# Convolution attention: values in column quarters, row sums as matmuls of their own, and a new order of the work around them

## The reference, cut to what matters

```python
def conv(x, ...):                                  # x: group norm of the input, (16, 128, 32, 32)
    q = einsum('bchw,oc->bohw', x, qW)             # 8 heads x 32, read as rows of 32
    k = einsum('bchw,oc->bohw', bn(dw_conv(x, kdwW, 2)), kW)     # 32 x 16 x 16
    v = einsum('bchw,oc->bohw', bn(dw_conv(x, vdwW, 2)), vW)
    attn = softmax(einsum('bnqd,bdl->bnql', q, k) / HEAD_DIM ** 0.5, axis=-1)   # over 256 keys
    ctx = einsum('bnql,bld->bnqd', attn, v)        # 8192 queries of an image, 32 values each
    return einsum('bchw,oc->bohw', ctx, oW)        # added to x
```

## Time and profile before

| | |
|---|---|
| time, median of 3 runs | 2161.94 us (2161.93 to 2164.02) |
| the profiled execution | 2174.15 us, its span 2172.4 us |
| PE, DVE, ACT busy | 1961.4, 1375.0, 989.7 us |
| mean granted TensorE clock | 0.967 |
| convolution attention | from 0 to 842.4 us of the span |

### The profile page before, as it was taken

How to read it: one execution, slowest core, us unless ns; L and a number is a source line. 1 busy time by engine, 2 the same in 40 slices (tenths; PEclk the granted TensorE clock), 3 DMA queues, 4 the chain that set the end, 5 groups by cost and what they waited for, 6 DMA issues and landing times. The chain is left out here.

```text
span 2172.4 us, 44335 instructions
## 1 busy us (share of the span) xinstructions
PE 1961.4 (90%) x11636; PEld 1466.1 (67%) x11636; DVE 1375.0 (63%) x3923; ACT 989.7 (46%) x2194; POOL 1029.3 (47%) x1367
## 2 busy tenths in 40 slices
PE   3999999999999998888898888887189999999997
PEld 2666666666666654665666666555189999999997
DVE  3676766767767665787788878876434444444443
ACT  0554555555455554444344333342045555555554
POOL 1221121212112111445554555555658888888887
PEclk9999999999999999999999999998589999999999
DMA  5322222222223222111111111111234444454454
GB/s 195 74 66 71 61 71 64 65 70 65 70 60 73 62 61 74 54 36 38 41 38 41 36 38 35 42 38 40 66 57 64 64 65 63 63 65 65 63 65 51
DMA packets 175423, 131.90 MB, mean 61 GB/s; under 512 B 33437, under 2 KB 164933, under 8 KB 175301
## 3 DMA queue, kind: packets, MB, share of 16 engines
q0 software_dynamic: 55808, 52.50, 15.1%
q1 hardware_dynamic: 118341, 77.16, 13.6%
q10 hardware_dynamic: 1152, 0.54, 0.1%
HBM read 31.47 MB, written 46.71 MB: 36 GB/s over the span
## 5 line engine op out<-in xcount | busy, mean ns | idle before, releaser
L1664 POOL DMA_INDIRECT out<-f_y,f_rows x272 | 424.1, 1559 | 45.5 <-POOL f_waited L1662 41.7
L447 DVE TENSOR_REDUCE neg_max<-s_bank 128x2 f32<-128x512 f32 x512 | 329.5, 685 | 133.5 <-PE s_bank L715 131.4
L1727 DVE SCALAR_TENSOR_TENSOR f_hidden<-f_silu,f_rows,f_h_bank 128x341 f32<-128x341 f32 x272 | 155.4, 571 | 307.6 <-ACT f_silu L1696 279.7
L567 ACT ACTIVATE probsT<-st_bank 128x512 f32<-128x512 f32 x512 | 276.6, 593 | 133.9 <-PE st_bank L733 133.6
L1096 POOL DMA_INDIRECT routed<-a_rows,a_target_idx x256 | 253.2, 989 | 68.6 <-issue 68.3
L335 POOL TENSOR_TENSOR waited<-nothing 128x1 int32<-128x1 int32 x64 | 12.1, 189 | 514.0 <-DVE q_low L436 514.0
L1473 PE MATMUL a_score_bank<-t_eT,t_gT 128*128 128x512 f32 x512 | 252.4, 617 | 1.2 <-DVE a_val L1140 1.2
L745 PE MATMUL o_bank<-probsT,v_ones 128*64 128x512 f32 x1024 | 248.0, 605 | 0.0
L1775 PE MATMUL f_y_bank<-w,f_hiddenT 114*128 (+1 forms) x1632 | 230.8, 277 | 1.3 <-ACT f_hiddenT L1688 1.3
L715 PEld LDWEIGHTS s_bank<-k_stack,q_stack 96*128 96x128 f32 x1024 | 141.9, 193 | 113.4 <-issue 94.0
L733 PE MATMUL st_bank<-q_stack,k_stack 98*128 98x512 f32 x512 | 214.0, 484 | 0.6 <-ACT probsT L567 0.5
(11 more groups left out here) (210 smaller groups left out, 3591.7 us busy)
## 6 DMA issues: line engine op xcount, KB each, us to landing
q_stack<-q_high SPq DMA_DIRECT2D x512, 64.0 KB, 2.3
f_rows<-routed SPq DMA_DIRECT2D x272, 66.0 KB
q_stack<-q_low POOLq DMA_DIRECT2D x256, 64.0 KB, 2.6
out<-X SPq DMA_DIRECT2D x16, 512.0 KB, 3.2
X<-in_x SPq DMA_DIRECT2D x1, 6144.0 KB, 22.1
out<-f_y,f_rows POOLq DMA_INDIRECT x272
q_stack<-max_rows SPq DMA_DIRECT2D x256, 4.0 KB
routed<-a_rows,a_target_idx POOLq DMA_INDIRECT x256
```

Of the source, the lines that this page charges most:

```text
L447: dve.tensor_reduce(neg_max[:, i % 2, CT * j:CT * (j + 1)], s_bank[h % 2][:], AX_X, ALU.max, negate=True).then_inc(max_ready, 1)
L567: act.activation(probsT[:, i % 2, c, lt, :], st_bank[lt][:], ACT.Exp).then_inc(exp_done, 1)
L1664: pool.indirect_dma_start(out=out, out_offset=bass.IndirectOffsetOnAxis(ap=rows[:, i, TOKEN:TOKEN + 1].bitcast(I32), axis=0), in_=y[:, i, ...
```

## The change

- The values go out in quarters: two pairs (an "octet", four chunks) at once, each chunk on 32 columns of its own quarter of `o_bank`. `values` runs in even iterations, for two pairs that are finished.
- The row sums come from matmuls of their own, `row_sums`, in odd iterations: the stationary operand has ones in one of 32 columns and zeros elsewhere, a different column for each octet of an image, and all four octets accumulate in one bank, `sum_bank`. Once per image ACT copies it out (`evacuate_sums`), PE turns it (`turn_sums`, end of i = 2) and DVE takes the reciprocals (`invert_sums`).
- The context is turned once per octet (end of odd iterations), and ACT, not DVE, takes it out (`evacuate_turned`, to `raw`). DVE scales half an image at a time (`scale`, i = 3 and i = 5 of the next period), and `project` of an image follows at i = 5 and i = 7 of the next period; `add_output` at i = 6 and at the end of i = 7.
- `m_bank` gives its bank to `sum_bank`; the maxes are turned into the first quarter of `c_bank`, with waits between the two uses.
- The convolution computes keys once and values, 64 columns, in two column halves at the same time (five taps and four); DVE adds the halves with a second operation. The copies of the keys are made in `split_keys`.
- `probsT` holds four pairs, `q_high` and `q_low` two groups of queries instead of four.
- On PE scores of rows 2 and 3 follow the second shifted scores at once; then come convolution or queries, then values or row sums, then a projection, then the turning. The statistics move to i = 2 (one half) and i = 4, `group_norm` to the end of i = 0.

```diff
+        sum_bank = ps("sum_bank", [P, COLS])
+        m_bank = c_bank[:, 0, :]
...
+                    dve.tensor_tensor(kv[:, slot, :], kv[:, slot, :], front[0:KV, 0:L], ALU.add).then_inc(kv_ready, 1)
...
+                def invert_sums(b):
+                    dve.wait_ge(sums_turned, b + 1)
+                    dve.reciprocal(rsum[:].rearrange("p (j c n) -> p j c n", j=OCTETS, c=OCTET_CHUNKS),
+                                   c_bank[:].rearrange("p n (c j) -> p j c n", j=QUAD)[:, 0:OCTETS]
+                                   ).then_inc(rsum_ready, 1)
+                    dve.wait_ge(rsum_ready, b + 1)
+                def scale(b, k):
+                    dve.wait_ge(c_out, OCTETS * (b + 1))
+                    wait(dve, out_full, 2 * (b - 1) + k + 1)
+                    part = slice(ROWS * k, ROWS * (k + 1))
+                    dve.tensor_tensor(context[:, part, :], raw[:, part, :],
+                                      rsum[:, part].unsqueeze(2).to_broadcast([P, ROWS, KD]), ALU.mult
+                                      ).then_inc(scaled, 1)
...
-                            normalise(*turned)
                         turning = pair(b, slot, i + LEAD - 1)
                         if has(turning[0]):
                             max_low(*turning)
+                        if i == 3 and has(b - 1):
+                            scale(b - 1, 0)
+                        if i == 5 and has(b - 1):
+                            scale(b - 1, 1)
+                        if i == 6 and has(b - 1):
+                            add_output(b - 1, 0)
...
+                        if i == 0 and has(new):
+                            group_norm(new)
+                        if i == 2 and has(b - 1):
+                            invert_sums(b - 1)
+                        if i == 2 and has(b + 2):
+                            half_stats(b + 2, 0)
+                        if i == 4 and has(b + 2):
+                            channel_stats(b + 2)
+                        if i == PAIRS - 1 and has(b - 1):
                             add_output(b - 1, 1)
-                        if i == PAIRS - 2 and has(b + 2):
-                            channel_stats(b + 2)
-                        if i == PAIRS - 1 and has(b):
-                            add_output(b, 0)
...
-                        wait(act, o_full, pair_no(b, i) - 1)
+                        wait(act, sums_full, octet_no(b, i // 2) - 1)
...
+                def evacuate_sums(b):
+                    act.wait_ge(sums_full, OCTETS * (b + 1))
+                    act.activation(sumT[:], sum_bank[:], ACT.Copy).then_inc(sums_out, 1)
+                def evacuate_turned(b, slot, o):
+                    act.wait_ge(c_full, octet_no(b, o) + 1)
+                    wait(act, scaled, 2 * b - (o < OCTETS // 2))
+                    rows = slice(2 * PAIR_ROWS * CT * o, 2 * PAIR_ROWS * CT * (o + 1))
+                    act.activation(raw[:, rows, :].rearrange("p (c n) d -> p n c d", c=OCTET_CHUNKS),
+                                   c_bank[:].rearrange("p n (c d) -> p n c d", d=KD), ACT.Copy).then_inc(c_out, 1)
...
-                            evacuate_context(*summed)
                         if i in Q_AT:
                             ahead, k = Q_AT[i]
                             if has(b + ahead):
                                 query_high(b + ahead, k)
+                        if i % 2 == 0 and has(summed[0]):
+                            evacuate_context(*summed)
+                        if i == 1 and has(b - 1):
+                            evacuate_sums(b - 1)
+                        if i % 2 and has(summed[0]):
+                            evacuate_turned(*summed)
...
+                    wait(pe, out_done, 2 * (b - 2))
...
+                    halves = ((4, 0, 1, 2, 7), (5, 3, 6, 8))
+                    for n in range(len(halves[0])):
+                        for part, taps in enumerate(halves):
+                            if n == len(taps):
+                                continue
+                            t = taps[n]
+                            di, dj = divmod(t, 3)
+                            out = front[KV * part:KV * (part + 1), 0:L].rearrange("p (i j) -> p i j", j=SIDE // 2)
+                            last = pe.matmul(out[:, di == 0:, dj == 0:], tap_w[:, t, :],
...
                     elif k == 2:
                         pe.wait_ge(q_low_done, Q_CHUNKS * b + 2)
+                        wait(pe, out_done, 2 * (b - 2) + 1)
...
-                    pe.wait_ge(ctx_done, pair_no(b, (k + 1) * PAIRS // 2 - 1) + 1)
-                    if k == 0 and has(b + 2):
-                        pe.wait_ge(gmean_ready, b + 3)
-                    elif k == 0 and has(b + 1):
-                        pe.wait_ge(q_low_done, Q_CHUNKS * (b + 1) + 3)
-                    elif k == 0:
-                        pe.wait_ge(head_done, head_no("e1"))
+                    pe.wait_ge(scaled, 2 * b + k + 1)
...
-                        for c in range(CHUNKS_PER_PAIR):
-                            last = pe.matmul(o_bank[HALF * c:HALF * (c + 1), :], v_ones[:, slot, lt, :],
-                                             probsT[:, i % 2, c, lt, :], start=(lt == 0), stop=(lt == LT - 1))
+                        for cc in range(OCTET_CHUNKS):
+                            i, c = divmod(cc, CHUNKS_PER_PAIR)
+                            last = pe.matmul(o_bank[QUAD * cc:QUAD * (cc + 1), :], v_rows[:, slot, lt, :],
+                                             probsT[:, (2 * o + i) % 4, c, lt, :], start=(lt == 0), stop=(lt == LT - 1))
...
+                def row_sums(b, o):
+                    if o == 0:
+                        wait(pe, sums_out, b)
+                    for lt in range(LT):
+                        for cc in range(OCTET_CHUNKS):
+                            i, c = divmod(cc, CHUNKS_PER_PAIR)
+                            last = pe.matmul(sum_bank[QUAD * cc:QUAD * (cc + 1), :], ones_at[:, o, :],
+                                             probsT[:, (2 * o + i) % 4, c, lt, :], start=(o == 0 and lt == 0),
+                                             stop=(o == OCTETS - 1 and lt == LT - 1), skip_group_check=True)
+                    last.then_inc(sums_full, 1)
+                def c_bank_free(b, i):
+                    turning = pair(b, 0, i + LEAD - 1)
+                    wait(pe, m_low_done, pair_no(turning[0], turning[2]) + 1 if has(turning[0]) else PAIRS * NB)
+                def turn_context(b, slot, o):
+                    pe.wait_ge(ctxT_full, octet_no(b, o) + 1)
+                    wait(pe, c_out, octet_no(b, o))
+                    wait(pe, rsum_ready, b)
                     for n in range(4):
-                        last = pe.transpose(c_bank[:, n, :], ctxT[:, i % 2, n * P:(n + 1) * P], ident[:])
+                        last = pe.transpose(c_bank[:, n, :], ctxT[:, o % 2, n * P:(n + 1) * P], ident[:])
                     last.then_inc(c_full, 1)
...
+                def turn_sums(b):
+                    pe.wait_ge(sums_out, b + 1)
+                    pe.wait_ge(c_out, OCTETS * (b + 1))
+                    for n in range(4):
+                        last = pe.transpose(c_bank[:, n, :], sumT[:, n * P:(n + 1) * P], ident[:])
+                    last.then_inc(sums_turned, 1)
...
-                        turned = pair(b, slot, i - 2)
-                        if has(turned[0]):
-                            turn_context(*turned)
+                        summed = octet(b, slot, i)
                         if has(scored[0]):
                             scores(*scored, 0)
                             scores(*scored, 1)
                         if has(turning[0]):
+                            if i == 3:
+                                wait(pe, rsum_ready, b)
+                            elif i % 2 == 0:
+                                before_last = octet(b, slot, i - 1) if i else octet(b - 1, 1 - slot, PAIRS - 1)
+                                if has(before_last[0]):
+                                    pe.wait_ge(c_out, octet_no(before_last[0], before_last[2]) + 1)
                             turn_maxes(*turning)
                         if has(b):
                             shifted_scores(b, slot, i, 1)
...
                             group_variances(new)
                         if i == PAIRS - 1 and has(b + 2):
                             group_means(b + 2)
...
-                        summed = pair(b, slot, i - 1)
-                        if has(summed[0]):
-                            values(*summed)
                         if has(scored[0]):
                             scores(*scored, 2)
                             scores(*scored, 3)
...
                             ahead, k = Q_AT[i]
                             if has(b + ahead):
                                 queries(b + ahead, k)
-                        if i == 3 and has(b - 1):
+                        if i % 2 == 0 and has(summed[0]):
+                            values(*summed)
```

(13 more changed lines are left out.)

194 lines of the change are left out of this document (94 added, 100 removed).

## The result

The changed kernel takes 2191.47 us (median of 4 executions, 2189.27 to 2194.87) against 2161.93 for the kernel before (4 executions, 2156.71 to 2164.02): a ratio of 1.0137, 95% interval 1.0115 to 1.016. It is slower by 1.4%, where 2148, 0.6% less, was forecast. The profiled executions stand 2193.1 to 2172.4 us in span.

What follows compares the result with a forecast made beforehand. PE sets the pace (busy 48.49 of 49.22 us per image). Iterations sum to 48.5 us, -0.65 per image, -10 us over 15 images; ends -4.0; about -14 in all, so 2161.94 goes to 2148; 8-in-10 range 2130 to 2203.

Steps and rivals of the forecast that it cites:

- the right two waits: Each iteration: row 3 of scores waits for DVE's row 1 bank, second shifted scores for exponentials; 0.41 us per iteration.
- leaves 41: Image 0: 48.5 less two projections, two blocks and 0.4 leaves 41 us against 47.43 before, so -6.4.
- +4.4: Stage end after the last values: 10.7 us after the change against 6.3 before.
- rival B: Values and row-sum blocks: quarters don't run four at once, 2203 to 2368; chances 0.13 (2167 to 2205), 0.10 above.
- Convolution and group means: Per image: convolution in column halves -1.6 us; idle gap at group means (i = 7) gone, -0.7 us.
- 2.7 us for the whole part: Each iteration from first shifted scores to end of rows 2 and 3's scores: 2.7 us, 2.29 without waits.
- Queries ahead of the block: Even iterations: queries, four records of 256 columns, add 0.85 us to the 4.57 of part and block.
- i = 3, "+0.15": DVE blocks on the turned sums at end of i = 2, making i = 3's first reduction 0.15 us late.
- i = 6, "+0.4": Queries at i = 6 wait for DVE's first half of the residual addition: 3.1 against 2.7 us, +0.4.
- C: ACT handovers or bank shared by maxes and context cost 0.3 us more in half the iterations: 2158 to 2167; chance 0.18.
- A: The forecast itself, whole kernel: 2148, with 2132 to 2157 for sizes within it; chance 0.47.
- D: Waits at rows of scores don't come: 3.3 us per image less, 2096, partly below 2130; chance 0.07.

Runs made afterwards that it cites:

- e10: Kernel before with only the column-halved convolution and the statistics in halves at i = 2 and i = 4; ratio 0.9866, image 46.78 us.
- e3: Changed kernel with two DVE steps reordered: half statistics ahead of reciprocals at i = 2, residual addition at start of i = 6; ratio 1.0066.
- e12: Changed kernel with each values or row-sums block in two halves, before the first scores and before the scores of rows 2 and 3; ratio 0.9869.
- e8: Changed kernel with the turned context copied out of PSUM by DVE at the start of even iterations, not by ACT; ratio 1.0092.
- e4: Kernel before with only the convolution in column halves and the statistics at i = 4; ratio 0.988.
- e1: Changed kernel with the block between second shifted scores and scores of rows 2 and 3, ACT's evacuations ahead of the queries'; ratio 1.0094.
- e5: e1 with the context turned right behind the row sums, plus e3's DVE order; ratio 1.0073.
- e11: e5 with each block in two halves and the reciprocals ahead of the statistics again at i = 2; ratio 0.9873.
- e9: Changed kernel with only the first half of each block moved, ahead of the first scores; second half stays behind convolution and queries; ratio 1.023.

## Why the prediction was wrong

The forecast had the right two waits and the wrong price for them, and so the wrong sign. The step that failed is the one that nets the gains of the convolution and the group means against the waits. All the rest of the change was put at +1.6 us per image by iterations (by terms +1.75: transposes -1.1, waits of the part +2.3, shared output bank and reciprocal +0.55); it costs +3.4 (e10 against after). The second step that failed is the ends, where "leaves 41" and "+4.4" carried the waits and the clock of a full image over to places that have less work to cover them.

Of the miss, 2191.5 - 2148 = 43.5 us, 34.7 lie in the span (2193.1 against 2172.4 - 14 = 2158.4). The other 8.8 are the step that took the profile's distance from the median (12.2 before) as unchanged; after, it is 3.4. The 2174.15 of the profile before isn't one of the four executions behind 2161.93; it lies beside that kernel's medians on two chips of this study (2175.14 and 2176.18) and not beside those on the two others (2158.5 and 2160.7), so the 12.2 may be a distance between chips. The chip of that profile isn't recorded.

- **Quarters (rival B): refuted, and the step was right.** Block 1.86 for 1.87. The Trainium skill (TensorE: Matmul & The Clock Gate, Part 3) measured 3.07 times for four tiles, there along the rows, which would have made an estimated 2.44 of a block. The trace doesn't bear that out for columns: four column quarters lose nothing to two halves.
- **Convolution and group means: right.** -2.4 alone (e10) for -2.3.
- **"2.7 us for the whole part": the mechanism was right, its terms too small.** Measured 2.81 (i = 4) and 2.88 (i = 5). By the maxes, i = 5: shifted scores 0.57 for my 0.47, 0.54 to the first reduction as priced, two reductions 1.29 for 1.3, and then 0.48 for 0.35 until PE is through the last scores. By the exponentials, i = 4: the first starts 0.86 after the shifted scores (I had 0.6 to 0.8) and the scores start at 2.33 (2.0 to 2.2).
- **Queries ahead of the block: 0.85 was too little.** 428.29 to 429.25 is 0.96. I gave the convolution 0.1 for going over to another shape and forgot it here. With it i = 0 and i = 4 miss by 0.15 and 0.20.
- **i = 3, "+0.15": failed, +0.54.** I had the reciprocal at 0.25 and the first reduction 0.15 late. The reciprocal of 128x64 takes 0.56, the statistics 0.69 stand behind it, and the first reduction (471.72) starts 1.60 after the first shifted scores, against 1.11 at i = 5 and 0.99 at i = 6: 0.5 to 0.6 late. The earlier trace rows had a 128x8 one at 0.20; I didn't scale it. e3 takes 0.55 back.
- **i = 6, "+0.4": failed by 0.21 more**: queries at 3.20 for 3.1, and the change of shape. e3 takes 0.54 back.
- **i = 5, +0.27:** the part by 0.18, the projection 1.82 for 1.72. i = 7 was met (6.92 for 6.95), i = 1 and i = 2 missed by 0.15 and 0.21, which the first two terms cover.

Together that is 50.2 - 48.5 = +1.7 per image, 24 us over the fourteen from image 1 to 14. The rest lies in the ends:

- **Image 0, "leaves 41": failed, 46.70.** I took two blocks and two projections off a full image and left the waits and the clock as in a later one. With less work between them the waits grow (0.57 and 0.70 us of idle PE), and the granted clock is 0.90 over the image, 0.60 under the convolution. That is +5.7. Its start came 1.4 earlier than I had it.
- **The last image and the tail: +12.0, where the sum had -0.65 + 4.4.** From the end of the last values (851.12) to the end of the stage 14.0 for 10.7: the reciprocal starts 4.95 after them for 3.9, it takes 0.56 for 0.25, the scaling 1.28 until PE starts for 1.1, and the projection 3.67 for 2.0, the last at clock 0.53. Before that, one block of values runs at 0.52 (+1.7), the second shifted scores, with no scores between, wait 0.44, 0.71 and 0.71 us for exponentials, and the head waits 0.44 for the addition.

With 24 us for the images, 5.7, 8.2 and -1.4 this makes 36.6, what the second layer's start shows (22.8 for -14); about 2 come back in later layers.

How much of the ends was waits and clock, and how much the change itself, e12 shows. With both waits covered its image 0 takes 42.77, 3.9 less than after; 1.55 of that lies at i = 1 (6.60 for 8.15), where the convolution runs at full clock. Its last image with the tail takes 56.6, 7.5 less than after and 4.5 more than before, where the sum had +3.75: that part of the sum holds for a kernel without the waits. The tail stays longer in every kernel with row sums of their own (56.6 us at least, against 52.0 before and in e10).

Of the rivals C comes nearest: the waits ate all. But it was priced up to 2167, for 0.3 us more in half of the iterations, and of its two mechanisms the shared bank costs nothing that the starts show, while the turned context's handover alone is worth 0.12 us of an iteration at most (e8). No rival held that several terms would miss by 0.1 to 0.5 in the same direction, which eight iterations and sixteen images then multiply. Smaller slips of the working: i = 6 is 5.42 + 0.4 = 5.82, not 5.87; the tail's terms add up to 10.6, not 10.7; and "faster" got 0.57, although A and D together have 0.54.

Open: in all kernels of this study, the time after the second layer's first matmul is 4 to 11 us more than the kernel before has by its median and the 842.84 of its one profile. That profile lies 12 us above its median, so the comparison may be at fault and not the kernels; e4 shows it too, which has none of the new blocks. The profiles point to the chips: after that matmul the kernels on two chips take 1321 to 1325 us (e1 to e4, e12), those on the two others 1330 to 1345 (e5 to e11), and the profile before takes 1329.6, like the latter. A profile of the kernel before on each chip would settle it; there is none.

## What to carry to other kernels

When an engine is fully busy, work that stands between a producer and its consumer is cover, and moving it away turns it into a wait, even if the same instructions remain. Find for each place where PE alternates with ACT and DVE which chain it waits on (here two), and cut the long work so that each has a piece of it; covering one can just move the wait or make it worse (e1 -0.4, e9 +1.6, e12 -3.4 us per image). Sum a period from start to start with every change of shape in it, and price the first and the last period by themselves, since what is missing there is just the cover.

## What the hardware showed that I had not expected

- Four column quarters of float32 matmuls run at once without loss: a wave of four records of 128*32 every 0.43 us, as a wave of two of 128*64.
- Next to a change of the tile shape the same work takes 0.1 to 0.15 us more: a half block of two waves takes 0.99 (2 x 0.43 = 0.86), one of four 1.86 (1.72), the queries ahead of a block 0.96 (0.85), the scores behind a block 0.58 (0.48 behind shifted scores). That the change of shape is the reason is my reading; no run changes the shape alone.
- Short waits of PE, off the steady state, can be followed by the low clock: 0.49 us idle, then 3.45 us at 0.52; 1.91 us idle, then 3.66 us at 0.53. It isn't fixed: in e3 the same block of values follows 0.48 us of idle time and takes 1.92 us at a granted clock of 1.00, and in e12 the same projection follows the same idle time and runs in its full-clock time, also at 1.00. PE in order of time, e12:

```profile
801.07 1.98 PE L727 MATMUL front<-context,owT 128*128 128x512 f32 x4 [1.91 <-DVE context L495]
```

From here the ends, other than the periods, can be priced only to within 2 us for each such place.
